# Self-attention's input loaded a second time in turned layout, and normalised in place with row tables of mean and deviation

## The chip, the cores and the metric

The kernel runs on one core of one Trainium2 chip. The metric is device microseconds (us) from the start to the end of one execution, and the time of a kernel is the median of its runs. One further execution is taken by the hardware profiler. Its rows name the engines PE (TensorE matmul), PEld (TensorE weight load), DVE (VectorE), ACT (ScalarE), POOL (GpSimd) and SP (SyncE, which here only issues DMAs).

## The reference

One decoder layer in float32: 2048 tokens (32 sequences of 64) of width 512.

```
x = x + self_attention(layernorm(x), w_q, w_k, w_v, w_o)           # 32 heads of 16
x = x + cross_attention(layernorm(x), ctx, pos, mask, Wq, Wk, Wv, Wo)  # 32 heads, 8 key/value heads of 128, rotary
x = x + linear(layernorm(x)) + bias + per-sequence and shared LoRA

def layernorm(x): return (x - mean(x)) / sqrt(var(x) + 1e-5)       # over the 512 features, no scale or offset
def self_attention(x, ...):                                        # q, k, v = x @ w.T
    return (softmax(q @ k.T / 4) @ v) @ w_o.T
```

The change is in how `layernorm(x)` of the first line reaches the matmuls.

## The kernel before

A matmul contracts over partitions, so the normalised tokens are needed turned: features on partitions, tokens along the row. Each float32 operand is split into a rounded part (`hi`) and a rest (`lo`), and a product is three matmuls (`product3`, L72 to L79) for each of KC = 4 chunks of 128 features. So every product of 128x512 outputs is 12 matmuls.

There are 2048 tokens: TILES = 16 tiles of 128, or NB = 4 blocks of 512 (TPB = 4 tiles each). The order of work is written out by hand, one program for each engine, tied by semaphores; `need(engine, semaphore, value)` is a wait.

The stage before the change's place is `KeysAndValues`: the keys and values of cross-attention from the context. It is `body(b)` for blocks b = 0 to 3, and in each for i = 0 to 7: PE does `keys(b, i)` (12 matmuls) and `values(b, i)` (12 matmuls). DVE rotates the keys in three instructions (`rotate`), POOL adds two of their terms (L313), ACT copies the values out of PSUM (`copy_values(b, i)`, L340), and SP stores both to DRAM (L257, L262). Keys have four output buffers `k_out`; values have two, `v_out`, so that the copy of values i waits until the store of values i-2 has landed (`v_stored`), and PE's `values(b, i)` waits for the copy of i-2. In blocks 1 and 2 the tokens `x_sb` are loaded tile by tile and DVE collects their statistics. At i = 0 of block 3 `finish_vector` and `finish_scalar` make `mv` (mean and variance) and `rstd` (one over the deviation) of all tiles: column t holds tile t, and partition p its token p.

Self-attention's first stage then goes tile by tile, t = 0 to 15. Before the change a tile passes five steps:

- DVE `normalise_tile(t)` (L156) writes `xn`, one of two buffers, from `x_sb`.
- PE `turn_tile(t)` (L687) turns it by four 128x128 transposes into a PSUM bank `ps_t`, of which there are two. It stands ahead of `values(t - 1)` in PE's program.
- ACT `tile_parts_hi(t)` (L808) rounds the bank into `xt_hi`.
- DVE `tile_parts_lo(t)` (L943) writes the rest into `xt_lo`.
- PE `values(t)` multiplies both by the value weights (12 matmuls), and ACT copies the result to `v1` (L812).

The first two tiles are prepared beside the last keys and values of block 3. Between tiles 8 to 12 stand the first projections of queries and keys (12 matmuls each) and the first scores. After tile 15 the attention's loop begins. Its first softmax (`exponentials(0, ...)`, L782) waits for `values(15)`, because its output buffer lies where the value weights are. DVE, ACT and POOL process each step of it, and PE's `turn(0)` (L659) waits for POOL's `p_pn` (L1031). POOL's part between the stages is to fill two buffers `v_x` with zeros (L1046) and to place values in them (L1039).

Of the kernel before, what the change touches and what calls it, by code (L numbers as in the profile page):

```python
# [26 lines left out]
P = 128  # L27
# [146 lines left out]
class KeysAndValues:  # L174

    def __init__(self, nc, m, base, banks, x, norm1, ident, drams, wv1_hi, wv1_lo):
# [40 lines left out]
        c_in0 = [m.sem(f"p1_c_in0_{c}") for c in range(KC)]  # L218
# [8 lines left out]
        self.wv1_ready = wv1_ready  # L227
# [7 lines left out]
        def sync(sp):  # L235
            for c in range(KC):
                sp.dma_start(c_raw[0][:, c, :], ctx_dram[:, c, 0:BLOCK]).then_inc(c_in0[c], 16)
                if c > 0:
                    sp.dma_start(raw["v"][:, c, 0:BLOCK], wv_dram[:, c, 0:BLOCK]).then_inc(v_raw_in[c], 16)
            sp.dma_start(ident[:, :], ident_dram).then_inc(id_in, 16)  # L240
            for c in range(KC):
                sp.dma_start(raw["v"][:, c, BLOCK:NKV], wv_dram[:, c, BLOCK:NKV]).then_inc(v_raw_in[KC], 16)
            sp.wait_ge(c_ready, KC)
            for i in range(KVH):
                sp.dma_start(raw["k"][:, :, i * D2:(i + 1) * D2], wk_dram[:, :, i * D2:(i + 1) * D2]).then_inc(k_raw_in[i // (KVH // NH)], 16)
# [1782 lines left out]
```

## Time and profile before

| | |
|---|---|
| median of 3 runs | 1423.76 us (1423.26 to 1425.62) |
| the profiled execution's own time | 1413.3 us |
| its span in the profile | 1411.1 us |
| PE busy | 1379.6 us, 98% |
| DVE busy | 1021.5 us, 72% |
| POOL busy | 529.2 us, 37% |
| ACT busy | 440.7 us, 31% |
| TensorE clock granted, mean | 0.996 of full |

The span is the time between the first and the last recorded instruction; the profiled execution took 2.2 us more than its span. A busy PE share counts overlapping spans of pipelined matmuls once, so what a matmul costs in a dense stretch is read from the distance between two starts and not from its duration.

### The profile page before, as it was taken

The page shows a single profiled execution, that of the slowest core. Times are in us where ns is not written, and L with a number is a line of the kernel's source. Part 1 is how long each engine was busy: PE and PEld are TensorE (multiplying, and loading weights), DVE is VectorE, ACT ScalarE, POOL GpSimd, SP SyncE. Part 2 cuts the span into 40 slices and gives each one's busy share as a digit, 9 for nine tenths or more (in the row PEclk, how much of TensorE's full clock was granted, in tenths as well). Part 3 has the DMA queues.
Part 4 walks back from the last instruction along what each step waited for, and adds up shares of the span by engine and source line. Part 5 has one row for each costly group of instructions (what it writes and reads, how often), then busy time and mean ns, then how long its engine had stood idle before and what let it go on. Part 6 is the DMA issues. An engine that isn't in the chain of part 4 may idle for free.

```text
span 1411.1 us, 27857 instructions
## 1 busy us (share of the span) xinstructions
PE 1379.6 (98%) x11552; PEld 1146.4 (81%) x11552; DVE 1021.5 (72%) x1476; ACT 440.7 (31%) x751; POOL 529.2 (37%) x457
## 2 busy tenths in 40 slices
PE   8999999999997799999999999999999999999999
PEld 6888888788886688888888888888888888888787
DVE  3755553788989977767767767777777777778765
ACT  5311233666657442122122122113123122122432
POOL 4422310444344524344344344344344344342131
PEclk9999999999999999999999999999999999999999
DMA  8654220000005012012011012011011011002011
GB/s 268 218 180 148 99 89 1 18 3 25 10 3 166 16 34 73 16 46 61 16 46 60 16 46 60 16 46 54 22 46 48 28 46 46 31 16 89 30 53 67
DMA packets 78859, 83.03 MB, mean 59 GB/s; under 512 B 9824, under 2 KB 50928, under 8 KB 78480
## 3 DMA queue, kind: packets, MB, share of 16 engines
q1 hardware_dynamic: 68832, 63.16, 14.3%
q10 hardware_dynamic: 9360, 17.04, 3.9%
q8 instruction: 93, 1.52, 0.5%
q0 software_dynamic: 544, 1.06, 0.3%
q14 instruction: 30, 0.25, 0.1%
HBM read 58.17 MB, written 23.07 MB: 58 GB/s over the span
## 4 chain that ended last, share of the span: by engine, by line
PE 60%; POOL 3%; DVE 1%; ACT 0%; issue 0%; ACTq 0%
PE p_ps_y L1272 6%; PE p_ps_y L1273 6%; PE p_ps_y L1274 6%; PE p_ps_qk L75 4%; PE p_ps_s L1233 3%; PE p_ps_qk L77 3%; PE p_ps_qk L76 3%; POOL p_wo_lo L1196 3%; PE p_ps_s L1244 2%; PE p_ps_s L1272 2%; PE p_ps_s L1274 2%; PE p_ps_s L1273 2%; PE p_ps_o L76 2%; PE p_ps_o L75 2%; PE p_ps_s L75 2%; PE p_ps_o L77 2%
## 5 line engine op out<-in xcount | busy, mean ns | idle before, releaser
L1650 POOL TENSOR_TENSOR p_q_rot<-p_q_rot,p_rb 128x512 f32<-128x512 f32 x128 | 167.2, 1306 | 310.7 <-DVE p_rb L171 310.7
L1272 PE MATMUL p_ps_y<-p_wo_hi,p_o_hi 128*128 128x512 f32 x384 | 151.2, 394 | 2.0 <-DVE p_o_lo L1526 1.3
L1273 PE MATMUL p_ps_y<-p_wo_lo,p_o_hi 128*128 128x512 f32 x384 | 149.5, 389 | 0.0
L1274 PE MATMUL p_ps_y<-p_wo_hi,p_o_lo 128*128 128x512 f32 x384 | 149.4, 389 | 0.0
L75 PE MATMUL p_ps_qk<-p_xt_hi,p_wq_hi 128*128 128x512 f32 x312 | 126.8, 406 | 0.9 <-DVE p_xt_lo L1550 0.9
L1031 POOL TENSOR_TENSOR p_pn<-p_p,p_inv 128x512 f32<-128x512 f32 x64 | 66.1, 1063 | 154.2 <-DVE p_inv L920 152.0
L1535 DVE TENSOR_TENSOR x_sb<-p_ps_y,x_sb 128x512 f32<-128x512 f32 x96 | 66.4, 692 | 77.0 <-PE p_ps_y L1274 76.0
L77 PE MATMUL p_ps_qk<-p_xt_hi,p_wq_lo 128*128 128x512 f32 x312 | 122.0, 391 | 0.0
L76 PE MATMUL p_ps_qk<-p_xt_lo,p_wq_hi 128*128 128x512 f32 x312 | 121.8, 390 | 0.0
L1380 ACT ACTIVATE p_pt_hi<-p_ps_s 128x512 fp32r<-128x512 f32 x64 | 34.9, 597 | 257.8 <-PE p_ps_s L1244 257.7
L1386 ACT ACTIVATE p_o_hi<-p_ps_s 128x512 fp32r<-128x512 f32 x64 | 34.7, 595 | 230.0 <-PE p_ps_s L1259 230.0
L1272 PEld LDWEIGHTS p_ps_y<-p_wo_hi,p_o_hi 128*128 128x128 f32 x384 | 72.1, 188 | 20.0 <-POOL p_wo_lo L1196 3.7
L1656 POOL TENSOR_TENSOR p_v_lo<-p_v_in,p_v_hi 128x512 fp32r<-128x512 f32 x32 | 41.3, 1292 | 124.6 <-ACT p_v_hi L1371 124.6
L169 DVE TENSOR_TENSOR p_q_rot<-p_ps_qk,p_cos_t 128x512 f32<-128x512 f32 x64 | 43.9, 686 | 59.2 <-PE p_ps_qk L77 57.3
L313 POOL TENSOR_TENSOR p_k_out<-p_k_out,p_rb 128x512 f32<-128x512 f32 x32 | 45.4, 1418 | 105.1 <-DVE p_rb L171 105.1
L1274 PEld LDWEIGHTS p_ps_y<-p_wo_hi,p_o_lo 128*128 128x128 f32 x384 | 72.1, 188 | 15.1
L1273 PEld LDWEIGHTS p_ps_y<-p_wo_lo,p_o_hi 128*128 128x128 f32 x384 | 72.1, 188 | 14.7 <-issue 0.2
L1643 POOL TENSOR_TENSOR p_s<-p_s,p_inv 128x512 f32<-128x512 f32 x64 | 65.5, 1044 | 34.7 <-DVE p_inv L1502 34.7
L1375 ACT ACTIVATE p_s<-p_s 128x1024 f32<-128x1024 f32 x32 | 34.0, 1063 | 117.1 <-DVE p_s L1494 117.1
L75 PEld LDWEIGHTS p_ps_qk<-p_xt_hi,p_wq_hi 128*128 128x128 f32 x312 | 58.7, 188 | 14.1 <-DVE p_xt_lo L1550 1.3
L77 PEld LDWEIGHTS p_ps_qk<-p_xt_hi,p_wq_lo 128*128 128x128 f32 x312 | 58.7, 188 | 12.8
L76 PEld LDWEIGHTS p_ps_qk<-p_xt_lo,p_wq_hi 128*128 128x128 f32 x312 | 58.9, 189 | 10.8
(262 smaller groups left out, 3774.1 us busy)
## 6 DMA issues: line engine op xcount, KB each, us to landing
k_scratch<-p_k_out SPq DMA_DIRECT2D x32, 256.0 KB, 2.1
p_raw<-in_wq SPq DMA_DIRECT2D x32, 256.0 KB, 3.2
p_raw<-in_wo SPq DMA_DIRECT2D x32, 256.0 KB, 2.7
p_k_t<-k_scratch ACTq DMA_DIRECT2D x32, 256.0 KB, 2.7
p_v_in<-v_scratch ACTq DMA_DIRECT2D x32, 256.0 KB, 2.8
v_scratch<-p_v_out SPq DMA_DIRECT2D x24, 256.0 KB, 2.6
x_sb<-in_x SPq DMA_DIRECT2D x16, 256.0 KB, 3.0
out<-p_y SPq DMA_DIRECT2D x16, 256.0 KB, 2.0
```

What stands on the lines that cost most here:

```text
L75: nc.tensor.matmul(out, lh, rh, start=(c == 0), stop=False)
L76: nc.tensor.matmul(out, lh, rl, start=False, stop=False)
L77: mm = nc.tensor.matmul(out, ll, rh, start=False, stop=(c == last))
L169: nc.vector.tensor_tensor(a[:, :], ps[:, :], cos, ALU.mult)
L313: nc.gpsimd.tensor_tensor(k_out[i % KOUT][:, :], k_out[i % KOUT][:, :], rb[i % 2][:, :], ALU.add).then_inc(k_added, 1)
L1031: nc.gpsimd.tensor_tensor(pn[:, u * PB:(u + 1) * PB, :, :].rearrange("p b j k -> p j b k"), part, scale.unsqueeze(3).broadcast_to([P, HALF ...
L1272: nc.tensor.matmul(ps_y[t][:, :], oh, w_hi["o"][h][:, :], start=(h == 0), stop=False)
L1273: nc.tensor.matmul(ps_y[t][:, :], oh, w_lo["o"][h][:, :], start=False, stop=False)
L1274: mm = nc.tensor.matmul(ps_y[t][:, :], ol, w_hi["o"][h][:, :], start=False, stop=(h == H - 1))
L1535: nc.vector.tensor_tensor(x[:, tile, :], ps_y[t][:, :], x[:, tile, :], ALU.add).then_inc(y_added, 1)
L1643: nc.gpsimd.tensor_tensor(part, part, inv[:, half * SETS:(half + 1) * SETS].unsqueeze(2).broadcast_to([P, SETS, SEQ]), ALU.mult).then_inc( ...
L1650: nc.gpsimd.tensor_tensor(q_rot[:, h, :], q_rot[:, h, :], rb[:, :], ALU.add).then_inc(q_added, 1)
```

## The change

The host passes `x` a second time, transposed (`xt`, features by tokens). Its four blocks of 1 MB are loaded into `xt_raw`, which is the memory that `xt_lo` takes later, at the beginning of block 3. PE turns `mv`'s means and `rstd` into rows (two small transposes, `turn_norm`), ACT copies them out (`copy_norm`), SP stores them to DRAM and loads them back as rows that are the same on all 128 partitions (`store_norm`, `load_rows`), 512 tokens in each. POOL subtracts the mean row in place (`centre_tile`), DVE multiplies by the deviation's row in place (`scale_tile`), ACT rounds and DVE takes the rest, both from SBUF. `normalise_tile` and `turn_tile` are gone. Four tiles instead of two are prepared beside block 3, and the steps for tile t run four tiles ahead of PE. Several buffers of `KeysAndValues` have other addresses.

```diff
@@ class KeysAndValues
+            def load_turned_tokens():
+                sp.wait_ge(c_ready, NB * KC)
+                sp.wait_ge(ready["k"], KVH)
+                sp.wait_ge(row_turned, NB)
+                for blk in range(NB):
+                    tokens = slice(blk * BLOCK, (blk + 1) * BLOCK)
+                    sp.dma_start(xt_raw[:, :, tokens], xt_dram[:, :, tokens]).then_inc(xt_in if blk == 0 else xt_rest_in, 16)
+            def store_norm():
+                sp.wait_ge(row_copied, NB + 1)
+                for i, scr in enumerate((mean_scr, rstd_scr)):
+                    sp.dma_start(scr.rearrange("o (t p) -> (o t) p", p=P), norm_rows[:, i, :]).then_inc(scr_out, 16)
+            def load_rows(blk, loaded):
+                sp.wait_ge(tables_out, 16 * 2 * NB)
+                sp.wait_ge(scr_out, SCR_OUT)
+                for rows_of, scr in ((mean_rows, mean_scr), (rstd_rows, rstd_scr)):
+                    sp.dma_start(rows_of[blk][:, :], scr[:, blk * BLOCK:(blk + 1) * BLOCK].broadcast_to([P, BLOCK])).then_inc(loaded, 16)
...
+                if b == NB - 1:
+                    load_turned_tokens()
                 for i in range(KVH):
                     store_keys(b, i)
                     store_values(b, i)
+                    if b == NB - 1 and i == 1:
+                        store_norm()
+                    if b == NB - 1 and i == 2:
+                        load_rows(0, near_rows_in)
+                        load_rows(1, near_rows_in)
...
             for i in range(2):
                 sp.wait_ge(v_stored[i], 16 * (NB - 1) * KVH // 2)
+            load_rows(2, far_rows_in)
+            load_rows(3, far_rows_in)
...
+            def copy_norm():
+                act.wait_ge(row_turned, NB + 1)
+                nc.scalar.activation(norm_rows[:, :, :], ps_r[0][0:TILES, 0:2 * P].rearrange("t (i p) -> t i p", i=2), ACT.Copy).then_inc(row_copied, 1)
...
+            def turn_norm():
+                pe.wait_ge(norm1.norm, 1)
+                for i, part in enumerate((norm1.mv[:, :, 0], norm1.rstd[:, :])):
+                    tr = nc.tensor.transpose(ps_r[0][0:TILES, i * P:(i + 1) * P], part, ident[:, :])
+                tr.then_inc(row_turned, 1)
...
                     extra(b, i)
+                    if b == NB - 1 and i == 1:
+                        turn_norm()
                     values(b, i)
@@ attention, tensor
-            def turn_tile(t):
-                need(pe, xn_ready, t + 1)
-                need(pe, tile_lo, t - 1)
-                for c in range(KC):
-                    tr = nc.tensor.transpose(ps_t[t % 2][:, c * P:(c + 1) * P], xn[t % 2][:, c * P:(c + 1) * P], ident[:, :])
-                tr.then_inc(transposed, 1)
...
             for t in range(TILES):
-                if 0 < t < TILES - 1:
-                    turn_tile(t + 1)
                 values(t)
@@ attention, scalar
             def tile_parts_hi(t):
-                need(act, transposed, t + 1)
+                need(act, scaled, t + 1)
                 need(act, kv.wv1_ready, KC)
+                need(act, kv.tables_out, 16 * 2 * NB)
+                if t == TPB:
+                    for stored in kv.k_stored[0:2]:
+                        need(act, stored, 16 * NB * KVH // 4)
...
+                nc.scalar.activation(xt_hi[:, :, t * P:(t + 1) * P], xt_raw[:, :, t * P:(t + 1) * P], ACT.Copy).then_inc(tile_hi, 1)
...
             for t in range(1, TILES):
-                if t > 1:
-                    tile_parts_hi(t)
+                if t + 3 < TILES:
+                    tile_parts_hi(t + 3)
                 copy_values(t - 1)
@@ attention, vector
-            def normalise_tile(t):
-                need(dve, transposed, t - 1)
-                norm1.apply(nc, xn[t % 2][:, :], t).then_inc(xn_ready, 1)
+            def scale_tile(t):
+                need(dve, centred, t + 1)
+                kv.wait_rows(dve, t // TPB)
+                xs, scale = xt_raw[:, :, t * P:(t + 1) * P], rstd_rows[t // TPB][:, t % TPB * P:(t % TPB + 1) * P]
+                nc.vector.tensor_tensor(xs, xs, scale.unsqueeze(1).broadcast_to([P, KC, P]), ALU.mult).then_inc(scaled, 1)
@@ attention, gpsimd
+            def centre_tile(t):
+                kv.wait_rows(pool, t // TPB)
+                xs, mean = xt_raw[:, :, t * P:(t + 1) * P], mean_rows[t // TPB][:, t % TPB * P:(t % TPB + 1) * P]
+                nc.gpsimd.tensor_tensor(xs, xs, mean.unsqueeze(1).broadcast_to([P, KC, P]), ALU.subtract).then_inc(centred, 1)
```

**SP's queue in block 3.** After the last store of block 2, the queue before is only stores of keys (`p_k_out`) and values (`p_v_out`):

```order
L253 DMA sin_scratch<-p_sin_t 128x512
L257 DMA k_scratch<-p_k_out_59 128x512
L262 DMA v_scratch<-p_v_out_72 128x4x128
L257 DMA k_scratch<-p_k_out_60 128x512
L262 DMA v_scratch<-p_v_out_73 128x4x128
L257 DMA k_scratch<-p_k_out_61 128x512
L262 DMA v_scratch<-p_v_out_72 128x4x128
```

And of the change:

```order
L267 DMA sin_scratch<-p_sin_t 128x512
L300 DMA p_xt_raw<-in_xt 128x4x512 x4
L271 DMA k_scratch<-p_k_out_67 128x512
L276 DMA v_scratch<-p_v_out_80 128x4x128
...
L305 DMA mean_scratch<-p_norm_rows 16x128
L305 DMA rstd_scratch<-p_norm_rows 16x128
L271 DMA k_scratch<-p_k_out_69 128x512
L276 DMA v_scratch<-p_v_out_80 128x4x128
L312 DMA p_mean_rows_52<-mean_scratch 128x512
L312 DMA p_rstd_rows_56<-rstd_scratch 128x512
L312 DMA p_mean_rows_53<-mean_scratch 128x512
L312 DMA p_rstd_rows_57<-rstd_scratch 128x512
```

Four 1 MB loads stand ahead of all of block 3's stores, and the rows' loads between the stores of i = 2 and i = 3.

**POOL, from the last adds of block 3 on.** Before, two adds, the zeros and the first placing of values:

```order
L313 TENSOR_TENSOR p_k_out_61<-p_k_out_61,p_rb_57 128x512
L313 TENSOR_TENSOR p_k_out_62<-p_k_out_62,p_rb_58 128x512
L1046 MEMSET p_v_x 128x1024 x2
L1039 COPY p_v_x<-p_v 64x4x4x16 x2
```

In the change (L357 is the add, L1112 the centring):

```order
L357 TENSOR_TENSOR p_k_out_67<-p_k_out_67,p_rb_65 128x512
L1112 TENSOR_TENSOR p_xt_raw<-p_xt_raw,p_mean_rows_52 128x4x128 x2
L357 TENSOR_TENSOR p_k_out_68<-p_k_out_68,p_rb_66 128x512
L1112 TENSOR_TENSOR p_xt_raw<-p_xt_raw,p_mean_rows_52 128x4x128
L357 TENSOR_TENSOR p_k_out_69<-p_k_out_69,p_rb_65 128x512
L1112 TENSOR_TENSOR p_xt_raw<-p_xt_raw,p_mean_rows_52 128x4x128
L357 TENSOR_TENSOR p_k_out_70<-p_k_out_70,p_rb_66 128x512
L1112 TENSOR_TENSOR p_xt_raw<-p_xt_raw,p_mean_rows_53 128x4x128 x4
L1126 MEMSET p_v_x 128x1024 x2
```

Sixteen instructions of centring are added, the first four between the adds of block 3.

**ACT, where block 3 ends.** Before, the copy of the last values, then the copy of tile 0's values (L812), then tile 2's rounding (L808):

```order
L340 ACTIVATE p_v_out_73<-p_ps_s 128x512
L812 ACTIVATE p_v<-p_ps_o 128x512
L808 ACTIVATE p_xt_hi<-p_ps_y 128x4x128
L812 ACTIVATE p_v<-p_ps_qk 128x512
L808 ACTIVATE p_xt_hi<-p_ps_y 128x4x128
```

In the change (L385, L866 and L862 are the same three):

```order
L385 ACTIVATE p_v_out_81<-p_ps_s 128x512
L862 ACTIVATE p_xt_hi<-p_xt_raw 128x4x128
L866 ACTIVATE p_v<-p_ps_o 128x512
L862 ACTIVATE p_xt_hi<-p_xt_raw 128x4x128
L866 ACTIVATE p_v<-p_ps_qk 128x512
```

The rounding now stands ahead of the copy, and it is that of tile 4.

## Rows read from the trace of the kernel before

**Rows 1.** The page's busy time by engine.
```profile
PE 1379.6 (98%) x11552; PEld 1146.4 (81%) x11552; DVE 1021.5 (72%) x1476; ACT 440.7 (31%) x751; POOL 529.2 (37%) x457
```

**Rows 2.** PE's waits in the first 400 us, second longest (total, times, longest).
```profile
PE p_ps_qk L659 <- POOL p_pn L1031: 1.7, 1, 1.7
```

**Rows 3.** Instruction groups of PE, 182 to 249 us (count, busy us, mean ns).
```profile
L687 PE MATMUL p_ps_y<-ident,p_xn 128*128 128x128 f32 x64 | 9.5, 272 | 0.0
```

**Rows 4.** PE's timeline around three of the tiles (start us, duration us).
```profile
182.17 1.03 PE L687 MATMUL p_ps_y<-ident,p_xn 128*128 128x128 f32 x8
185.78 0.39 PE L75 MATMUL p_ps_o<-p_wv_hi,p_xt_hi 128*128 128x512 f32 x1
188.50 0.60 PE L687 MATMUL p_ps_y<-ident,p_xn 128*128 128x128 f32 x4
191.71 0.60 PE L687 MATMUL p_ps_y<-ident,p_xn 128*128 128x128 f32 x4
...
246.02 0.39 PE L75 MATMUL p_ps_qk<-p_wv_hi,p_xt_hi 128*128 128x512 f32 x1
248.52 0.39 PE L77 MATMUL p_ps_qk<-p_wv_hi,p_xt_lo 128*128 128x512 f32 x1
```

**Rows 5.** DVE's timeline: `rstd` made, and the last rotation's last instruction.
```profile
149.16 0.25 DVE L143 RECIPROCAL rstd<-sd 128x16 f32<-128x16 f32 x1 [1.39 <-ACT sd L153]
183.78 0.68 DVE L171 TENSOR_TENSOR p_rb<-p_ps_s,p_sin_t 64x512 f32<-64x512 f32 x1
```

**Rows 6.** Windows (engines' busy us, PEclk, DMA share, GB/s): full queues.
```profile
62.00:64.00 2.00, 2.00 (x11) 1.65 (x10) 1.67 (x3) 0.00 (x0) 0.00 (x0) 1.00 1.07 399
...
101.00:103.00 2.00, 2.00 (x10) 1.65 (x10) 1.94 (x4) 0.00 (x0) 0.27 (x1) 1.00 0.88 253
```

**Rows 7.** DMAs issued 60.5 to 61.2 us: time from issue to landing.
```profile
v_scratch<-p_v_out SPq DMA_DIRECT2D x1, 256.0 KB, 8.8
```

**Rows 8.** SP's timeline: end of block 2, first and third stores of block 3.
```profile
142.98 0.58 SPq L253 DMA_DIRECT2D sin_scratch<-p_sin_t  x1
147.76 0.32 SPq L257 DMA_DIRECT2D k_scratch<-p_k_out  x1
...
159.53 0.43 SPq L262 DMA_DIRECT2D v_scratch<-p_v_out  x1
```

**Rows 9.** ACT's timeline: copies of block 3, i = 2 and 4; first softmax.
```profile
157.88 0.60 ACT L340 ACTIVATE p_v_out<-p_ps_s 128x512 f32<-128x512 f32 x1 [4.32 <-PE p_ps_s L77]
168.76 0.60 ACT L340 ACTIVATE p_v_out<-p_ps_s 128x512 f32<-128x512 f32 x1 [4.32 <-PE p_ps_s L77]
...
248.94 0.60 ACT L812 ACTIVATE p_v<-p_ps_qk 128x512 f32<-128x512 f32 x1 [2.12 <-PE p_ps_qk L77]
249.56 1.28 ACT L782 ACT_TABLE_LOAD   x1
```

**Rows 10.** SP's timeline, two issues, and their time to landing (KB, us).
```profile
1299.05 0.43 SPq L1767 DMA_DIRECT2D p_w_raw<-in_wf  x1
1299.52 2.09 SPq L1768 DMA_DIRECT2D p_bias<-in_bias  x1
...
p_w_raw<-in_wf SPq DMA_DIRECT2D x1, 1024.0 KB, 8.9
...
p_bias<-in_bias SPq DMA_DIRECT2D x1, 256.0 KB, 9.8
```

**Rows 11.** POOL's timeline: the adds of block 3, i = 4 and 7.
```profile
168.22 1.80 POOL L313 TENSOR_TENSOR p_k_out<-p_k_out,p_rb 128x512 f32<-128x512 f32 x1 [3.64 <-DVE p_rb L171]
...
184.54 1.29 POOL L313 TENSOR_TENSOR p_k_out<-p_k_out,p_rb 128x512 f32<-128x512 f32 x1 [4.15 <-DVE p_rb L171]
```

**Rows 12.** DVE's groups, 140 to 240 us (count, busy us, mean ns, idle before).
```profile
L156 DVE TENSOR_SCALAR p_xn<-x_sb,mv,rstd 128x512 f32<-128x512 f32 x16 | 10.3, 649 | 0.0
L943 DVE TENSOR_TENSOR p_xt_lo<-p_ps_y,p_xt_hi 128x512 fp32r<-128x512 f32 x14 | 9.6, 689 | 28.9 <-ACT p_xt_hi L808 28.9
L410 DVE TENSOR_TENSOR p_wv_lo<-p_raw_k,p_wv_hi 128x512 fp32r<-128x512 f32 x4 | 2.8, 693 | 0.1
```

More of the change, by code:

```diff
@@ L217, in __init__ @@
         v_raw_in = [m.sem(f"p1_v_raw_in{i}") for i in range(KC + 1)]
-        c_in0 = [m.sem(f"p1_c_in0_{c}") for c in range(KC)]
+        c_in0 = [m.sem(f"p1_{n}") for n in ("c_in0_0_and_xt", "c_in0_1_and_xt_rest", "c_in0_2_and_near_rows", "c_in0_3_and_norm_and_far_rows")]
+        xt_in, xt_rest_in, near_rows_in, far_rows_in = c_in0
+        scr_out = far_rows_in
+        XT_IN, XT_REST_IN, NEAR_ROWS_IN, SCR_OUT, FAR_ROWS_IN = 16 + 16, 16 + 16 * (NB - 1), 16 + 16 * 4, 16 + 16 * 2, 16 + 16 * 2 + 16 * 4
         c_in = m.sem("p1_c_in")
@@ L506, in body @@
                     extra(b, i)
+                    if b == NB - 1 and i == 1:
+                        turn_norm()
                     values(b, i)
@@ L544, in attention @@
         o_hi, o_lo = m.sb("o_hi", [P, BLOCK], F32R), m.sb("o_lo", [P, BLOCK], F32R)
-        xn = [nc.alloc_sbuf_tensor_at(f"p3_xn{i}", [P, HIDDEN], F32, offset=xn_at + 4 * HIDDEN * i) for i in range(2)]
+        xt_raw = nc.alloc_sbuf_tensor_at("p3_xt_raw", [P, KC, TOKENS], F32, offset=base + 32 * 1024)
+        mean_rows, rstd_rows = ([nc.alloc_sbuf_tensor_at(f"p3_{n}_rows{b}", [P, BLOCK], F32, offset=base + at * 1024) for b, at in enumerate(places)]
+                                for n, places in (("mean", (12, 152, 142, 146)), ("rstd", (20, 170, 144, 148))))
         assert xn_at == base + 170 * 1024 and nc.sbuf_base == xn_at + 2 * 4 * HIDDEN
@@ L948, in beside_values @@
                     norm1.finish_vector(nc, dve)
+                if b == NB - 1 and i == KVH - 3:
+                    scale_tile(0)
+                    scale_tile(1)
                 if b == NB - 1 and i == KVH - 2:
-                    normalise_tile(0)
-                    normalise_tile(1)
+                    tile_parts_lo(0)
+                    scale_tile(2)
+                    tile_parts_lo(1)
+                if b == NB - 1 and i == KVH - 1:
+                    scale_tile(3)
+                    tile_parts_lo(2)
+                    tile_parts_lo(3)
             kv.vector(dve, beside_values)
-            need(dve, kv.tables_out, 16 * 2 * NB)
-            for stored in kv.k_stored[0:3]:
-                need(dve, stored, 16 * NB * KVH // 4)
+            scale_tile(TPB)
             for t in range(TILES):
-                if 0 < t < TILES - 1:
-                    normalise_tile(t + 1)
-                tile_parts_lo(t)
+                if t + TPB + 1 < TILES:
+                    scale_tile(t + TPB + 1)
+                if t + TPB < TILES:
+                    tile_parts_lo(t + TPB)
                 if 3 <= t < 6:
@@ L1041, in place_values, with beside_keys @@
                 pool.wait_ge(v_placed, it + 1)
-            kv.gpsimd(pool)
+            def centre_tile(t):
+                kv.wait_rows(pool, t // TPB)
+                xs, mean = xt_raw[:, :, t * P:(t + 1) * P], mean_rows[t // TPB][:, t % TPB * P:(t % TPB + 1) * P]
+                nc.gpsimd.tensor_tensor(xs, xs, mean.unsqueeze(1).broadcast_to([P, KC, P]), ALU.subtract).then_inc(centred, 1)
+            def beside_keys(b, i):
+                if b == NB - 1 and i == KVH - 4:
+                    centre_tile(0)
+                    centre_tile(1)
+                if b == NB - 1 and KVH - 4 < i < KVH - 1:
+                    centre_tile(i - KVH + 5)
+            kv.gpsimd(pool, beside_keys)
             need(pool, kv.v_done, NB * KVH)
+            for t in range(TPB, 2 * TPB):
+                centre_tile(t)
             for buffer in v_x:
@@ L1047, in _ @@
             pool.wait_ge(zeroed, 2)
+            for t in range(2 * TPB, TILES):
+                centre_tile(t)
+            pool.wait_ge(centred, TILES)
             place_values(0)
@@ L1961, in decoder_layer @@
         sin_scr = nc.dram_tensor("sin_scratch", (P, TOKENS), F32, kind="Internal").ap()
+        mean_scr, rstd_scr = (nc.dram_tensor(n + "_scratch", (1, TOKENS), F32, kind="Internal").ap() for n in ("mean", "rstd"))
         xs, ident = m.sb("x_sb", [P, TILES, HIDDEN]), m.sb("ident", [P, P])
```

78 lines of the change are left out of this document (45 added, 33 removed).

## The prediction

> **What bounds the kernel now.** I read the page's busy shares first: PE is busy 98% of the span and no other engine over 72% [rows 1]. Busy time of pipelined matmuls hides small gaps, so the waits come next: in the first 400 us, after the start, PE's longest wait is 1.7 us, for POOL in the first softmax [rows 2]. So from the beginning of block 3 to that softmax every other engine, and every transfer, is hidden, and an instruction taken off PE moves all that follows. What PE's instructions cost there is to be read from the distance of their starts. Tile 0's product starts at 185.78 and tile 1's transposes at 188.50: 12 matmuls in 2.72 us, 0.227 each. The last tile's twelve, which have no transposes ahead, start at 246.02 and 248.52: 2.50 plus one step of 0.227 is again 2.72. But from one tile's transposes to the next's it is 191.71 - 188.50 = 3.21 [rows 4]. So four transposes with the break in the stream that they make cost 3.21 - 2.72 = 0.49 us. The first eight, ahead of the last values of block 3, cost 185.78 - 182.17 - 2.72 = 0.89.
>
> **Removed: 64 transposes.** There are 64 in the stretch [rows 3]: a run of eight and 14 runs of four. 0.89 + 14 x 0.49 = **7.75 us** off PE. DVE's 16 normalisations of 0.65 us [rows 12] go too, and are worth nothing, since PE doesn't wait for DVE.
>
> **Added on PE: two small transposes** of 16 columns after `keys(3, 1)`. No row shows this form. From 0.49 for four and 0.89 for eight, one costs 0.10 and a break 0.09 (0.49 - 4 x 0.10), so two cost **0.30**; the bounds are 0.1 (the break alone) and 0.54 (two whole durations of 0.272). They also wait for `rstd`, made at 149.41 [rows 5]. Block 3's step is 5.44 us and the copy of values 2 starts at 157.88 [rows 9], so PE ends `values(3, 2)` at about 157.7 and `keys(3, 1)` 3 x 2.72 earlier, at 149.5. The margin is 0.1 us, so this wait is 0 to 0.3 us. I take 0.
>
> On the new clock `values(3, 7)` starts at 182.17 and ends at 184.9, where tile 0 begins, and tile t begins at 184.9 + 2.72 t up to t = 8.
>
> **Added on SP's queue: 4 x 1.05 = 4.2 MB ahead of block 3's stores.** They are issued from about 143.6 on, when SP used to wait until 147.76 [rows 8], so SP's time is free. The stores' landing is not. Full queues moved 253 to 399 GB/s [rows 6]. Loads and the first two stores are 4.7 MB: 12 to 19 us, so the first store of values lands between 155 and 163. A third bound comes from block 1, where a store behind 2 MB of loads landed after 8.8 us [rows 7]; twice that from 148.1 is 165.7. The copy of values 2 waits for it. It was due at 157.88, and PE needs it at `values(3, 4)`, which starts 2.72 ahead of the copy at 168.76, at 166.0; less the copy's 0.60, the landing may be as late as 165.4 [rows 9]. Cost: 0 by the first two bounds, 0.3 by the third. I take 0, because this load has the shape and rate of the context's, from whose stretch the 253 is.
>
> **The row tables.** The two norm stores go behind 5.2 MB: they land by 143.6 + 21, about 165. SP then issues four row loads, 1.05 MB, behind the stores of i = 2, and these land at L = 164 (the faster rate, and the store's issue at 159.5) to 172.5. A broadcast load's price is bounded by the bias, which landed 0.5 + 0.9 = 1.4 us after the 1 MB load issued before it, though its issue took 2.1 us instead of 0.4 [rows 10]; four such issues would move L to 177 at worst. POOL is free for centring when the add of i = 4 ends, at 170.0 [rows 11]. From L on: two centrings of 1.8, two scalings of 0.69, the rotation of i = 6 (2.1), and the rest of tile 0 (0.69), in all L + 7.8. PE needs it at 184.9, so L may be 177. Cost 0, at the limit 0. The far rows go out when block 3's stores have landed, at about 188, and land by 195. Tile 8 is needed at 206.7 and takes 3.8 us of steps: 8 us to spare. SP's weight loads for the projections stand 2 us later, and PE wants them only from tile 8 on.
>
> **Added on POOL: 16 centrings.** POOL's 128x512 subtraction of this shape isn't in the trace. Its adds take 1.29 us alone and 1.80 beside DVE [rows 11]; a DVE instruction with two SBUF inputs kept its 0.69 beside them [rows 12]. Either is under PE's 2.72 for a tile. The Trainium skill, GPSIMD Engine Reference, Engine selection, says to give elementwise work to VectorE, since GpSimd takes about twice as long with two inputs. The ratio here, 1.29 to 0.69, agrees, and by that rule the change is wrong by 16 x 0.6 = 9.6 us if POOL were on the path. By the rows it is not, but for one place, which is next.
>
> **What is late next: ACT at the stage's start.** The rounding of tile 4 now stands ahead of the copy of tile 0's values, and PE's `values(2)` at 190.3 waits for that copy. The chain: POOL's add of i = 7 ends at 185.8; centring of tile 4, 1.29 to 1.80; scaling 0.69; rounding 0.60; copy 0.60; and four hand-overs of 0.08 (DVE ends at 184.46, POOL starts at 184.54 [rows 5, 11]). It ends at 189.3 to 189.8, and at 190.3 if the add takes 1.80 as well. So there is 0 to 1.0 us to spare; were the centring 2.8 us, PE would wait 1 us. DVE takes over what it had: rest 0.69 and scaling 0.69 instead of 0.65, half of its 2.72.
>
> **Given back later?** The first softmax can't start before tile 15's product: the copy at 248.94, then ACT's table load at 249.56 [rows 9]. Both follow PE, so PE's 1.7 us wait moves with the stage and stays as long.
>
> **The sum.** 7.75 - 0.30 = 7.45; for the two waits with almost no margin (bounds 0.3 and 1.0) I take off 0.25: **7.2 us**. The profiled execution took 1413.3 us (span 1411.1, 2.2 around it) and becomes 1406.1. The median of runs is 10.5 us above it, an offset that the change doesn't touch: 1423.76 - 7.2 = **1416.6 us**.
>
> **Rivals.**
> 1. *Stores queue behind the loads.* If the queue gives under 230 GB/s, the landing is past 165.4 and PE stops at `values(3, 4)`. At 200 GB/s it lands at 167 to 168, and PE waits 2 to 3 us; with the wait of ACT's start 1 to 5 us in all: 1418 to 1421.5. For it speaks the third bound [rows 7], against it both rates [rows 6]. Chance 0.12, half of it still beyond the 0.2%.
> 2. *The transposes are worth their durations.* 64 x 0.272 = 17.4 us [rows 3], less 0.5 and 0.25: 1407.1. For it speaks only that the run is broken at each place; the starts speak against it. The Trainium skill, TensorE: Matmul & The Clock Gate, Part 4, gives about 275 ns for a transpose in a kernel's context, most of it access latency; the row's 272 agrees as a duration, and by it the sum would be 17 us. In this dense stream the latencies overlap. Chance 0.03.
> 3. *No change.* Something not tied to PE sets the first softmax's start, and PE waits 7 us longer there: 1423.8. The chain of rows 9 speaks against it. Chance 0.04.
> 4. *Slower: the row tables are late.* Four broadcast loads read one DRAM row into 128 partitions, after stores of the same bytes. PE waits L + 7.8 - 184.9 us at tile 0. It eats the gain at L = 184 and passes the bound for slower at L = 187. At L = 190 it is 12.9 us: 1429.5. It takes 15 us more than my latest estimate from rates. The bias speaks against. Chance 0.04.
>
> My forecast holds the other 0.77.
>
> **How the numbers follow.** 0.2% is 2.85 us, about what runs of this kernel can tell from no change. Faster: 0.77 + 0.06 + 0.03 = 0.86. Same: 0.06 + 0.04 = 0.10. Slower: 0.04. The forecast's own range: at best 7.75 - 0.1 = 7.65, at worst 7.75 - 0.54 - 1.0 - 0.3 - 0.3 = 5.6, and 1.2 us of spread between runs on either side: 1414.9 to 1419.4. The 8 in 10 range takes in part of rival 1: 1414.5 to 1420.5.
>
> **What would show it.** The transposes' line gone, and tile after tile starting 2.72 us apart. Tile 0 at about 184.9 plus 0.3. The first block 3 store of values landing before 165.4, and no PE wait at `values(3, 4)`. The first row loads landing before 177. No PE wait on `v_copied` at tile 2, or one under 1 us. The same PE wait of 1.7 us at the first softmax. Wrong would be: a PE wait in block 3 for ACT's copy, or for DVE's rest of tile 0 or 4, or a centring of more than 2.7 us.

## The result and the profile after

The changed kernel takes 1442.2 us (median of 5; before 1423.76, median of 5): 1.0128 times the time before, 95% interval 1.0107 to 1.0149. It is slower by 18 us, where 7.2 us less was forecast. Its profiled execution took 1435.3 us, which is one of the five.

The page after. PE's busy time is hardly different [rows 1], but its share fell from 98% to 96%.

```profile
span 1432.7 us, 27787 instructions
...
PE 1381.8 (96%) x11490; PEld 1145.6 (80%) x11490; DVE 1039.5 (73%) x1476; ACT 441.3 (31%) x752; POOL 554.7 (39%) x473
```

PE's waits after (total, times, longest). Before, the longest in the first 400 us, after the start of the kernel, was 1.7 us [rows 2].

```profile
PE p_ps_s L705 <- issue: 10.5, 8, 1.9
...
PE p_ps_o L75 <- ACT p_v L866: 4.5, 2, 2.4
...
PE p_ps_qk L75 <- issue: 1.7, 1, 1.7
```

There are two new kinds behind the start. The copies of values (ACT, L866) belong to the stage that was changed. The waits inside the scores (L705) are in attention's loop, which the change didn't touch, and "issue" says that PE waited for nothing that the profile knows.

To place the loss I cut the span at three events that both kernels have: ACT's table load at i = 0 of block 3, the last copy of a tile's values, and the last placing of values (`p_v_x`, near the loop's end). ACT's timeline before, and the placings as a group (the range is that of their starts):

```profile
147.62 1.28 ACT L153 ACT_TABLE_LOAD   x1
```

```profile
L796 ACT ACTIVATE p_v_x<-p_v x32: 414/415/418, 208.6 to 432.3; 64x256 f32<-64x256 f32 x32
```

The same two views after:

```profile
148.56 1.28 ACT L153 ACT_TABLE_LOAD   x1
...
249.01 0.60 ACT L866 ACTIVATE p_v<-p_ps_qk 128x512 f32<-128x512 f32 x1 [2.12 <-PE p_ps_qk L77]
```

```profile
L843 ACT ACTIVATE p_v_x<-p_v x32: 413/415/417, 214.2 to 453.9; 64x256 f32<-64x256 f32 x32
```

With the last copy of before at 248.94 [rows 9] the **stage** (table load to last copy) is 101.32 us before and 100.45 after: 0.87 us won of 7.45. The **loop** (to the last placing) is 183.4 before and 204.9 after: 21.5 us lost. What follows is 978.8 in both. The table load itself comes 0.9 us later, behind one wait of 1.7 us put down to issue at 37.2. Between the two profiled executions that makes 0.94 - 0.87 + 21.53 = 21.6 us of span and 22.0 of time. The medians are only 18.4 apart, because the profiled executions were 10.5 us under their median before and 6.9 after. So there are two questions, and the larger is in a place where no instruction changed.

**The loop.** PE's timeline after, the scores of two turns (x: matmuls of the group). Each turn has 128 of these small matmuls.

```profile
278.07 1.25 PE L705 MATMUL p_ps_s<-p_k_x,p_q_x 32*64 32x64 f32 x97
280.47 0.49 PE L705 MATMUL p_ps_s<-p_k_x,p_q_x 32*64 32x64 f32 x31 [1.15 <-issue]
...
292.07 1.30 PE L705 MATMUL p_ps_s<-p_k_x,p_q_x 32*64 32x64 f32 x102
294.74 0.47 PE L705 MATMUL p_ps_s<-p_k_x,p_q_x 32*64 32x64 f32 x26 [1.36 <-issue]
```

The break moves: after matmul 93, 97, 102, 106, 111, 115, 120 and 124 in eight turns, then just behind the scores in two, then never. A wait for data would stay at one instruction. A break that moves by 4.5 matmuls a turn is tied to a count of instructions. Counted in the built program (no view shows this number; the windows below show 250 matmuls a turn, each with its weight load), a turn has 503 instructions on TensorE, the 128 matmuls with their weight loads are 256 of them, and 512 - 503 = 9 instructions are 4.5 matmuls.
Queue q8 in this quarter of a microsecond (packets, MB, share), and the window's own row:

```profile
q8 instruction: 1, 0.02, 23.6%
```

```profile
292.25:292.50 0.25, 0.25 (x39) 0.25 (x33) 0.12 (x1) 0.25 (x1) 0.25 (x1) 1.00 0.24 66
```

The same holds in the turns around it: packets at 263.75 and 278.0, PE on at 266.33 and 280.47. The change took 138 instructions off PE ahead of the loop (transposes, their weight loads and waits), and so moved where the pieces end. **Rival B**: the stalls come of data or work beside the loop.

A wait costs more than its length. Windows after, turn by turn:

```profile
278.07:292.07 14.00, 12.85 (x250) 10.79 (x244) 11.15 (x13) 7.36 (x12) 5.60 (x7) 1.00 0.14 40
292.07:307.92 15.85, 14.49 (x252) 11.99 (x245) 10.80 (x12) 7.35 (x12) 5.38 (x7) 0.89 0.01 2
...
412.69:425.39 12.70, 12.70 (x250) 10.77 (x244) 10.57 (x12) 7.36 (x12) 4.59 (x7) 1.00 0.01 3
```

The columns are the turn's length, busy time of PE, PEld, DVE, ACT and POOL, then the granted clock, DMA share and GB/s. A turn without a wait takes 12.70 us; one with 1.15 us of waiting takes 14.00; one with 1.36 takes 15.85, because the granted clock falls to 0.89 of full in it. After such a wait the 512-column matmuls stand 0.43 us apart (starts at 295.14 and 295.57) instead of 0.23, which is the 1.2 GHz level. Four turns have it (waits of 1.36, 1.71, 1.88, 1.73), 1.7 to 1.9 us each beyond the wait. So 12.6 us of waits (10.5 in the scores, 1.7 and 0.4 just behind them) and some 7 of clock make most of the 21.5.

**The stage.** PE's three waits in it, in its timeline, then the timelines of DVE and of POOL beside them (L998 scales, L1002 takes the rest, L1112 centres):

```profile
194.11 0.47 PE L75 MATMUL p_ps_o<-p_wv_hi,p_xt_hi 128*128 128x512 f32 x1 [2.44 <-ACT p_v L866]
...
209.27 0.47 PE L75 MATMUL p_ps_qk<-p_wv_hi,p_xt_hi 128*128 128x512 f32 x1 [1.13 <-ACT p_v L866]
...
214.34 0.47 PE L75 MATMUL p_ps_o<-p_wv_hi,p_xt_hi 128*128 128x512 f32 x1 [2.10 <-ACT p_v L866]
```

```profile
187.65 3.48 DVE L1002 TENSOR_TENSOR p_xt_lo<-p_xt_raw,p_xt_hi 128x512 fp32r<-128x512 f32 x2
191.05 3.44 DVE L998 TENSOR_TENSOR p_xt_raw<-p_xt_raw,p_rstd_rows 128x512 f32<-128x512 f32 x2
...
196.11 0.68 DVE L998 TENSOR_TENSOR p_xt_raw<-p_xt_raw,p_rstd_rows 128x512 f32<-128x512 f32 x1
...
201.11 1.77 DVE L998 TENSOR_TENSOR p_xt_raw<-p_xt_raw,p_rstd_rows 128x512 f32<-128x512 f32 x1 [2.51 <-POOL p_xt_raw L1112]
202.80 1.79 DVE L1002 TENSOR_TENSOR p_xt_lo<-p_xt_raw,p_xt_hi 128x512 fp32r<-128x512 f32 x1
```

```profile
188.84 6.80 POOL L1112 TENSOR_TENSOR p_xt_raw<-p_xt_raw,p_mean_rows 128x512 f32<-128x512 f32 x4
195.58 1.84 POOL L1126 MEMSET p_v_x<- 128x1024 f32 x2
199.79 12.71 POOL L1112 TENSOR_TENSOR p_xt_raw<-p_xt_raw,p_mean_rows 128x512 f32<-128x512 f32 x8 [2.36 <-DMA p_rstd_rows<-rstd_scratch]
```

From 188.84 to 195.6 and from 199.79 to 212.5 POOL centres without a break, and there a DVE instruction with two inputs in SBUF takes 1.72 to 1.79 us; beside POOL's fill with zeros the same instruction takes 0.68. Two things can have made ACT's copies late: this, or ACT's own queue, which stood still for the projections' weights, whose load now stands behind four loads of rows on SP:

```profile
192.85 0.63 ACT L862 ACTIVATE p_xt_hi<-p_xt_raw 128x512 fp32r<-128x512 f32 x1 [3.97 <-DVE p_xt_raw L998]
193.39 0.58 ACT L866 ACTIVATE p_v<-p_ps_o 128x512 f32<-128x512 f32 x1
...
200.63 0.63 ACT L670 ACTIVATE p_wq_hi<-p_raw_q 128x512 fp32r<-128x512 f32 x1 [2.69 <-DMA p_raw_q<-in_wq]
```

### The profile page after: what moved, and what is told of

The parts are those of the page before. It is cut to its first block, busy times and chain, and to the rows that moved or that the text cites. A ratio compares the mean times of both kernels' runs of the same rounds, so it can differ in the third digit from the quotient of the medians.

```text
span 1432.7 us, 27787 instructions
## 1 busy us (share of the span) xinstructions
PE 1381.8 (96%) x11490; PEld 1145.6 (80%) x11490; DVE 1039.5 (73%) x1476; ACT 441.3 (31%) x752; POOL 554.7 (39%) x473
## 4 chain that ended last, share of the span: by engine, by line
PE 60%; DVE 2%; POOL 2%; issue 1%; ACT 0%; ACTq 0%
PE p_ps_y L1355 6%; PE p_ps_y L1356 6%; PE p_ps_y L1357 6%; PE p_ps_s L1316 4%; PE p_ps_qk L75 4%; PE p_ps_qk L77 3%; PE p_ps_qk L76 3%; PE p_ps_s L1327 2%; PE p_ps_s L1357 2%; PE p_ps_s L1356 2%; PE p_ps_s L1355 2%; PE p_ps_o L76 2%; PE p_ps_o L75 2%; PE p_ps_o L77 2%; PE p_ps_s L75 2%; PE p_ps_s L76 2%
## 5 line engine op out<-in xcount | busy, mean ns | idle before, releaser
L357 POOL TENSOR_TENSOR p_k_out<-p_k_out,p_rb 128x512 f32<-128x512 f32 x32 | 46.3, 1448 | 100.9 <-DVE p_rb L171 99.5
```

The costliest lines, as they stand in the source:

```text
L357: nc.gpsimd.tensor_tensor(k_out[i % KOUT][:, :], k_out[i % KOUT][:, :], rb[i % 2][:, :], ALU.add).then_inc(k_added, 1)
```

## The experiments

**Four at once: the place in the stream, and who centres.** The edit that moves the place, in PE's program, ahead of each `keys` and `values` of blocks 1 and 2 (in the kernel before 118, 160 or 256 in all, spread in the same way):

```diff
+            PADS = [5, 5, 5, 5, 5, 5, 5, 5, 5, 5, 4, 4, 4, 4, 4, 4, 4, 4, 4, 4, 4, 4, 4, 4, 4, 4, 4, 4, 4, 4, 4, 4]
+
+            def pad(n):
+                for _ in range(2 * PADS[n] if n < len(PADS) else 0):
+                    pe.wait_ge(id_in, 16)
...
+                    pad(2 * ((b - 1) * KVH + i))
                     keys(b, i, (lambda c: need(pe, c_ready, b * KC + c + 1)) if i == 0 else (lambda c: None))
...
+                    pad(2 * ((b - 1) * KVH + i) + 1)
                     values(b, i)
```

Two such waits become one instruction: the page counts 27975 instructions with 118 more, 27857 before. The semaphore has its value from the kernel's start on, so that nothing is waited for. And the edit that moves the centring:

```diff
@@ attention, vector, scale_tile
-                need(dve, centred, t + 1)
                 kv.wait_rows(dve, t // TPB)
+                xs, mean = xt_raw[:, :, t * P:(t + 1) * P], mean_rows[t // TPB][:, t % TPB * P:(t % TPB + 1) * P]
+                nc.vector.tensor_tensor(xs, xs, mean.unsqueeze(1).broadcast_to([P, KC, P]), ALU.subtract).then_inc(centred, 1)
+                need(dve, centred, t + 1)
@@ attention, gpsimd
-            for t in range(TPB, 2 * TPB):
-                centre_tile(t)
...
-            for t in range(2 * TPB, TILES):
-                centre_tile(t)
```

The four centrings beside block 3 go from POOL in the same way.

*The change with 138 more instructions.* 

> The changed kernel, with 138 more instructions on TensorE's queue between the weight loads of blocks 1 and 2 (waits for a semaphore that has long had its value; four or five ahead of each keys or values), so that attention's loop begins at the place of the instruction stream at which it begins in the kernel before. Theory A (TensorE's instructions come in pieces of 256, and a stall comes when a whole piece lies in the dense run of small matmuls of one iteration; the change took 138 instructions away and so moved where the pieces end): the waits of 1.1 to 1.9 us put down to issue inside the scores of eight iterations (10.5 us together) go, the loop takes about 182 us again instead of 203, and the time falls from 1442 by about 20 to some 1422; what is left in the tile stage (4.5 us of TensorE's waits for the values' copies) stays. Rival B (the stalls come from the data in DRAM or SBUF, or from work beside the loop, which the change moved): they stay, and the time stays within 2 us of 1442. If the added instructions themselves cost 30 ns each, they would add 4 us.

*The kernel before with 118 more.* 

> The kernel before, with 118 such instructions on TensorE's queue in blocks 1 and 2, so that its loop begins at the place of the stream at which the changed kernel's begins (counted modulo 256). Theory A: the old kernel gets the changed kernel's stalls, put down to issue inside the scores at about matmul 93, 97, 102, ... 124 of eight iterations in a row, 1.1 to 1.9 us each, and is slower by 18 to 22 us, at about 1443. Rival B: nothing of the kind, within 2 us of 1424 (or up to 4 us above, were each added instruction 30 ns).

*The change, centring on VectorE.* 

> The changed kernel with the centring of each tile on VectorE instead of GpSimd, in one instruction more per tile there (about 0.69 us alone), nothing on GpSimd. Theory (GpSimd's centring back to back slows VectorE's instructions with two SBUF inputs from 0.69 to 1.78 us, and so the copies of the values behind them come late): VectorE's three passes over a tile take 0.69 us each, 2.1 together beside TensorE's 2.72, TensorE's waits for ACT in the second run of eight and behind go (5.7 us), and the time falls by 4 to 6 us; the count of TensorE's instructions hardly changes, so the stalls in the loop stay. Rival (what makes the copies late is ACT's own queue, or the loads of rows): the waits stay, 0 to 1 us.

*Both edits.* 

> Both edits. If both theories hold and the costs add, about 1442 less 20 less 5, some 1416 to 1418, and faster than the kernel before by 6 to 8 us, which is the saving that the transposes were worth. If either is wrong, its share is missing: 1422 (no gain from VectorE), 1437 (no gain from the place in the stream).

| | time | before, same chip | ratio (95%) | stage | loop |
|---|---|---|---|---|---|
| change + 138 | 1419.15 | 1423.86 | 0.9983 (0.9954 to 1.0012) | 100.6 | 182.9 |
| before + 118 | 1444.69 | 1423.86 | 1.0144 (1.0123 to 1.0166) | 101.3 | 203.0 |
| change, centring on VectorE | 1444.2 | 1423.86 | 1.0149 (1.0128 to 1.017) | 97.8 | 203.0 |
| both | 1419.32 | 1423.86 | 0.9963 (0.9945 to 0.998) | 97.9 | 182.9 |

The kernel before, with nothing but 118 waits that are already met, shows the changed kernel's stalls, at the same matmuls. Its timeline:

```profile
271.56 1.22 PE L651 MATMUL p_ps_s<-p_k_x,p_q_x 32*64 32x64 f32 x93 [0.33 <-ACT p_q_x L775]
273.49 0.62 PE L651 MATMUL p_ps_s<-p_k_x,p_q_x 32*64 32x64 f32 x35 [0.71 <-issue]
...
285.25 1.25 PE L651 MATMUL p_ps_s<-p_k_x,p_q_x 32*64 32x64 f32 x97
287.64 0.49 PE L651 MATMUL p_ps_s<-p_k_x,p_q_x 32*64 32x64 f32 x31 [1.15 <-issue]
```

And the changed kernel with 138 such waits has none of them: its scores are x128 in one group turn after turn, and its loop is as long as before the change. Rival B is out. These two places also fix the portion: the kernel before with 118 more and the change are 118 + 138 = 256 instructions apart (138 by the count in the program), and both stop at the same matmuls. A portion of 512 would put them 128 matmuls apart. A portion of 128 would give the kernel before a break at matmul 88 in turn 2 and 4.5 further in each turn behind it, and it has none.

Centring on VectorE wins 2.7 us of the stage (100.5 to 97.8). The 4 to 6 us expected of it were not seen in the times, nor the 6 to 8 us expected of both edits (4.5 by the medians): its ratio to the kernel before is 1.0149 where the change has 1.0128, and with the 138 it is 0.9963 where the padded change has 0.9983, intervals that overlap in both cases. The rows show what it does. VectorE's centring (L997), scaling (L1000) and rest take 0.69 each there, and up to 1.78 only where one of POOL's adds of block 3 is already running (here one from 183.71 on):

```profile
184.27 1.78 DVE L997 TENSOR_TENSOR p_xt_raw<-p_xt_raw,p_mean_rows 128x512 f32<-128x512 f32 x1
186.09 0.69 DVE L1000 TENSOR_TENSOR p_xt_raw<-p_xt_raw,p_rstd_rows 128x512 f32<-128x512 f32 x1
```

And the waits of that version, of ACT and of PE:

```profile
ACT p_wq_hi L670 <- DMA p_raw_q<-in_wq: 4.6, 1, 4.6
...
PE p_ps_o L75 <- ACT p_v L866: 1.8, 1, 1.8
PE p_ps_qk L75 <- ACT p_v L866: 1.6, 1, 1.6
```

What is left are 3.4 us of PE's waits where none was expected, and ACT's 4.6 for the weights.

**Two doses, and what else delays the copies.** The edit for the weights, on ACT and the same on DVE:

```diff
-                if 3 <= t < 6:
-                    split_hi(act, "qko"[t - 3], 0, done["q"], 0)
+                if 5 <= t < 8:
+                    split_hi(act, "qko"[t - 5], 0, done["q"], 0)
```

*The kernel before with 256 more.* 

> The kernel before, with 256 more instructions on TensorE's queue in blocks 1 and 2: over twice as many as the 118 that made it 20.8 us slower. Theory A (pieces of 256 instructions: what counts is the place modulo 256, and 256 more give the same place): no wait put down to issue inside the scores, and the time stays within 3 us of 1423.9, the added instructions' own cost included (the run with 118 had TensorE's first 140 us about as long as without). Rival (the added instructions themselves, or any move of the loop against the stream, cost the time): slower by 20 to 45 us.

*With 160 more.* 

> The kernel before, with 160 more. With 118 the first stall came in the third scores (iteration 2) at matmul 93 and moved by 4.5 a loop turn. Theory A: 42 instructions more are 21 matmuls less, so the piece ends at matmul 72 in iteration 2, 76, 81, 85, 90 in the next, without a stall as long as the place is under about 88 to 93; then stalls of 1.1 to 1.9 us at about 94, 99, 103, 108, 112, 117, 121, 126 in iterations 7 to 14: the stalls start four to five turns (some 60 us) later in the loop, as many of them as before, and the time is again 18 to 22 us above, at 1442 to 1446. If the stalls were tied to these iterations or to their place in time, they would come in iterations 2 to 9 again or not at all.

*The padded change, weights split later.* 

> The changed kernel with the 138 added instructions (1419.2 us), and the splitting of the projections' weights on ACT and DVE two tiles later, at t = 5 to 7 instead of 3 to 5. In the changed kernel ACT stood 2.7 us still for the query weights, whose load now stands behind four loads of rows, and the copies of values behind it were late. If that load is the cause of TensorE's waits for the copies (4.6 us in this version), most of it goes: 1415 to 1416. If it is VectorE's instructions slowed by GpSimd's centring (1.78 instead of 0.69 us each), which this edit leaves, TensorE's waits stay above 3 us and the time stays at 1417 to 1419.

*The same, centring on VectorE.* 

> The same with the centring on VectorE (1419.3 us without the later splitting; TensorE's waits for ACT's copies were 3.6 us, and ACT stood 4.6 to 4.8 us still for the query weights). With both causes gone TensorE's waits in the tile stage fall under 1 us and the time to 1415.5 to 1417, 7 to 8 us under the kernel before. If instead the rows of the last eight tiles are what is late (VectorE waited 2.9 us for them), 1 to 2 us of TensorE's waits stay: 1417 to 1418.

| | time | before, same chip | ratio (95%) | stage | loop |
|---|---|---|---|---|---|
| before + 256 | 1414.54 | 1413.62 | 1.0006 (0.9996 to 1.0015) | 101.3 | 182.6 |
| before + 160 | 1438.64 | 1413.62 | 1.0166 (1.0150 to 1.0181) | 101.3 | 208.9 |
| change + 138, late split | 1411.09 | 1413.62 | 0.9980 (0.9971 to 0.9989) | 97.3 | 183.5 |
| and VectorE | 1410.08 | 1413.62 | 0.9966 (0.9952 to 0.9980) | 95.9 | 182.9 |

The experiments ran on two chips, so each time is to be compared with its own column of the kernel before: 1413.6 us on the chip of this table, 1423.9 and 1424.6 on the other.

256 more change nothing (0.9 us, within the interval): the stalls come of the place and not of the number added, and the added waits cost nothing measurable. The number of packets on queue q8 fits that it carries TensorE's instructions, one more for 256 more. Its row on the page before, and with 256 more on TensorE:

```profile
q8 instruction: 93, 1.52, 0.5%
```

```profile
q8 instruction: 94, 1.54, 0.5%
```

With 160 the places are those that the count gives (72 in turn 2, and 4.5 more in each). One shorter wait of 0.65 comes at 72, where I expected none. At 76 and 81 there is none, and from 85 on, two turns sooner than I expected, every turn has one until the place has left the scores:

```profile
262.74 1.05 PE L651 MATMUL p_ps_s<-p_k_x,p_q_x 32*64 32x64 f32 x72 [0.32 <-ACT p_q_x L775]
264.44 0.85 PE L651 MATMUL p_ps_s<-p_k_x,p_q_x 32*64 32x64 f32 x56 [0.65 <-issue]
...
276.43 1.60 PE L651 MATMUL p_ps_s<-p_k_x,p_q_x 32*64 32x64 f32 x128
...
301.89 1.15 PE L651 MATMUL p_ps_s<-p_k_x,p_q_x 32*64 32x64 f32 x85
304.46 0.73 PE L651 MATMUL p_ps_s<-p_k_x,p_q_x 32*64 32x64 f32 x43 [1.42 <-issue]
```

By the same count the kernel before goes from 24 in turn 2 to 82.5 in its last turn, without a wait: it had stopped one step short. With 160 there are eleven waits in the scores, 15.5 us, where I expected eight, and the loop is 26 us longer. The expectation was right in the sign and in how the place moves, and wrong in where the stalls begin; the size, 25.0 us, is 3 us over its upper end.

The later split wins 3.3 us of the stage with POOL centring and 2.0 with VectorE. Of the 3.3, PE's waits are 1.7 (4.6 to 2.9). Much of the rest is clock: in the version without the later split the granted clock is 0.91 between 191 and 211 us, and with it 1.00 in the whole stage. One wait of 1.8 is left in the last version, for the copy of tile 0's values, behind the rounding of tile 4; I had expected under 1 us.

The times don't show these gains. The first version met neither of its expectations: 2.9 us of waits are left, and it is 2.5 us under the kernel before, less than either. The ratios to the kernel before are 0.9983 without and 0.9980 with the later split, and 0.9963 and 0.9966 with VectorE centring. The last version is 3.5 us under the kernel before where 7 to 8 were expected. Beside the profile of the kernel with 256 more, on the same chip, its stage is 5.4 us shorter, its start 0.5 and its part behind the loop 1.9 us longer.

**The copy ahead of the rounding.**

```diff
+                copy_values(t - 1)
                 if t + 3 < TILES:
                     tile_parts_hi(t + 3)
-                copy_values(t - 1)
```

*POOL centring.* 

> GpSimd centres, 138 added instructions, late splitting (as the version that was 2.5 us under the kernel before, with 2.9 us of TensorE's waits for copies in the tile stage), and ACT copies the values of tile t-1 before it rounds tile t+3 instead of after. The copies then wait for nothing but TensorE. If VectorE's slowed instructions (1.78 us) hurt only through ACT's order, the 2.9 us go and nothing takes their place: 4.5 to 5.5 us under the kernel before, stage 94.5 us long from ACT's table load to the last copy (before 101.3; changed kernel 100.5; this version without the edit 97.3). If VectorE is too slow for TensorE in itself (it has two passes of 1.78 and four of 0.7 in two tiles beside the projections' splitting), TensorE waits for the rest of a tile instead, 1 to 3 us: the stage stays at 96 to 97.5.

*VectorE centring.* 

> The same with the centring on VectorE (without the edit: 3.5 us under the kernel before, stage 95.9 us, one wait of 1.8 us for the copy of tile 0's values, which stood behind the rounding of tile 4). The wait goes: stage 94.1 us, which is 7.2 us less than before (forecast of the prediction's sum: 7.2 to 7.5), and the time some 5 to 7 us under the kernel before, 1 to 2 us of the stage's gain missing outside of it. Rival: the wait moves to the rest of tile 1 or 2 on VectorE, and the stage stays within 0.5 us of 95.9.

| | time | before, same chip | ratio (95%) | stage | loop |
|---|---|---|---|---|---|
| POOL centres | 1422.38 | 1424.63 | 0.9979 (0.9966 to 0.9991) | 98.3 | 183.9 |
| VectorE centres | 1416.7 | 1424.63 | 0.9945 (0.9931 to 0.9960) | 93.9 | 182.9 |

With POOL centring the wait moves: PE now stands for VectorE, which is too slow in itself, and the stage is 1.0 us longer than without the edit, 98.3 where at most 97.5 was expected. It is 4.4 us longer than with VectorE centring: 2.2 are waits, and in the 10 us from 217.8 on, in which the 2.0 us wait falls, the granted clock is 0.83. PE's waits there, 150 to 260 us:

```profile
PE p_ps_s L75 <- DVE p_wq_lo L684: 2.0, 1, 2.0
...
PE p_ps_o L75 <- DVE p_xt_lo L1009: 0.2, 1, 0.2
```

With VectorE centring PE waits for nothing in the stage. ACT's rows of that version:

```profile
157.96 1.28 ACT L153 ACT_TABLE_LOAD   x1
...
199.87 0.59 ACT L873 ACTIVATE p_v<-p_ps_o 128x512 f32<-128x512 f32 x1
...
251.82 0.60 ACT L873 ACTIVATE p_v<-p_ps_qk 128x512 f32<-128x512 f32 x1 [2.12 <-PE p_ps_qk L77]
```

The stage is 251.82 - 157.96 = 93.86 us, 7.46 less than before, and the kernel takes 1416.7 us, 7.9 less than before, where 5 to 7 was expected. That the two gains are so close is not shown to be more than chance: the part behind the loop alone differs between profiles by up to 3 us (last section).

## Why the prediction was wrong

**The step that failed is "Given back later?", which ended at the first softmax: the sum has no term for anything behind it.** I followed what comes behind the stage by its waits for other engines, and put the rest at nothing when every wait was accounted for. The loop had no wait put down to issue and no changed instruction, and lost 21.5 us. The sum's last step, "an offset that the change doesn't touch", didn't hold either, but to the good: the offset between profiled execution and median went from 10.5 to 6.9 us. Shown: added instructions alone bring the stalls to the old kernel (118, 160) or take them from the new one (138), and 256 do neither. Argued and not shown: that what PE stands for is the instruction packet 2.3 to 2.6 us before it goes on, why the bad places begin between matmul 82 and 85, and why there was a short wait at 72. No rival of mine held this. The nearest, numbers 3 and 4, ended at the stage.

**The terms on PE were right.** Transposes 7.75 less two small ones 0.30 is 7.45; the stage without waits gained 7.46. The two small transposes cost 0.24, not 0.30: the starts of every third matmul are 0.82 and 0.78 us apart around them instead of 0.68.

```profile
149.78 0.39 PE L75 MATMUL p_ps_s<-p_c_hi,p_wk_hi 128*128 128x512 f32 x1
...
150.57 0.27 PE L543 MATMUL p_ps_y<-ident,rstd 128*16 128x128 f32 x1
150.60 0.48 PE L75 MATMUL p_ps_s<-p_wv_hi,p_c_hi 128*128 128x512 f32 x1
...
151.38 0.40 PE L75 MATMUL p_ps_s<-p_wv_hi,p_c_hi 128*128 128x512 f32 x1
...
152.07 0.39 PE L75 MATMUL p_ps_s<-p_wv_hi,p_c_hi 128*128 128x512 f32 x1
```

Rival 2 (17.4 us by durations) is out.

**"A DVE instruction with two SBUF inputs kept its 0.69 beside them" was the second failed step.** POOL's adds of before came alone, and DVE's two-input instruction had started 0.05 us ahead of them (168.17 against 168.22 for i = 4); DVE kept 0.69 [rows 12] and it was POOL that took 1.80 instead of 1.29 [rows 11]. I read from that who suffers, when it only showed who had come first. Centrings back to back (a run of four and one of eight) come first nearly always. And DVE's rest used to read PSUM and SBUF, its normalisation one SBUF input; after the change all its instructions of the stage had two. The Trainium skill, SBUF — State Buffer, SBUF: two separate sides, says it as a rule: a VectorE instruction with two SBUF inputs and a GpSimd instruction that reads SBUF exclude each other, the first holds the ports to its end. The rows agree in kind: 1.77 to 1.79 against 0.68, and 0.68 beside the fill, which reads nothing. The price is a little under the sum of both instructions, 0.69 + 1.29 = 1.98. So "half of its 2.72" became 3.5 us a tile, over PE's step. "Late next: ACT at the stage's start" had the right place: by my count the copy of tile 0's values ended at 189.3 to 190.3, and it ended at 193.97 (0.9 us of it is the later start of the stage). Ahead of tile 4's rounding (192.85) stand two rests and one scaling of 1.7 us each on DVE, from 187.65 on, for 0.69 each; and POOL's add of i = 7, which waits for DVE's last rotation, started at 187.09 instead of 184.54 and took 1.79.

**"SP's weight loads for the projections stand 2 us later, and PE wants them only from tile 8 on"** looked past ACT. The conversion stood at t = 3 in ACT's program, the load was issued at 194.3 instead of 189.3 (5 us later, 0.9 of it the later start, and not 2), and ACT stood 2.69 us with the copies behind it. Its share depends on what else is cured: 3.3 us of the stage with POOL centring (about half of it clock), 2.0 with VectorE.

**The transfers held.** The first store of values let the copy of values 2 go at 160.33, inside 155 to 163 and under 165.4, so rival 1 fell. The near rows kept nobody waiting (rival 4 fell). The far rows landed by 199.79, not 195: POOL waited 2.4 us.

## What to carry to other kernels

When a change adds or removes instructions on an engine ahead of a dense loop, the loop's place in the instruction stream moves, and its time can change by more than the edit is worth: look for waits put down to issue whose place moves by a fixed count, and test with instructions that do nothing. Before elementwise work goes to GpSimd, count VectorE's instructions beside it that have two inputs in SBUF, and price them at nearly their own time plus that of the one they meet (here 1.77 us for 0.69 beside 1.29). A conversion of weights in the middle of a copying engine's program is a wait for its load.

## What the runs showed of the hardware

- TensorE's stalls repeat with every 256 instructions: 118 more cost 20.8 us, 160 cost 25.0, 256 cost 0.9 (within 0.2%). A bad place cost waits of 0.4 to 1.9 us a turn, and after the four longest 1.7 to 1.9 us in addition at the lower clock.
- Waits on a semaphore that has its value long since cost nothing measurable in a dense stream: 256 instructions of them in blocks 1 and 2, stage and loop as before.
- Centring beside nothing takes POOL 1.29 us, back to back beside DVE 1.59 to 1.74; DVE's two-input instruction takes 1.77 beside it.
- On the chip where the kernel before took 1423.9 or 1424.6 us, TensorE waits 3.1 to 5.9 us near 40 us for the first rotation, and ACT's table load of block 3 comes at 151.9 to 158.0. On the one where it took 1413.6 there is no such wait, and the load comes at 147.2 to 148.4. So most of the 10.5 us between the first profiled execution and the median probably lie in the start; the unchanged kernel has no profile beside the slower median, and this stays unshown.
- The part behind the loop was 978.8 us in both first profiles and 980.0 to 982.2 in the ten versions of the experiments. In the seven changed ones it takes 1.2 to 3.1 us off the gain. I have not found its cause; whether it is the place in the stream there as well is open.
